# Relative-position attention and a gated FFN on one core: transposes issued directly behind the scores of their slot

## The reference

```python
q, k, v = einsum('bsx,xMnd->Mbnsd', x, qkv)
a = einsum('bnsd,bntd->bnst', q, k) * 64**-0.5
a = softmax(a + where(rel >= 0, cumsum(rpe)[:, clip(rel)], -30000), -1)
x = layernorm(x + einsum('bnsd,ndx->bsx', einsum('bnst,bntd->bnsd', a, v), out_w))
xr, xk = mix of x and the token before it, with mu_r and mu_k
x = layernorm(x + sigmoid(xr @ W_r) * (square(relu(xk @ W_k)) @ W_v))
```

## Time and profile before

| | us |
|---|---|
| median of 3 runs | 1245.39 (1245.36 to 1245.45) |
| the profiled execution's own time | 1246.39 |
| its span | 1244.6 |
| PE busy | 1118.1 (90%) |
| POOL busy | 886.9 (71%) |
| DVE busy | 843.3 (68%) |
| ACT busy | 743.1 (60%) |

### The profile page before, as it was taken

The page is one execution under the profiler, slowest core; times in us unless marked ns, Lnnn a source line. Parts: engine busy times, 40 slices in busy tenths (PEclk is TensorE's granted clock), DMA queues, the critical chain, the costliest instruction groups (busy, mean ns, idle before and its releaser), DMA issues.

```text
span 1244.6 us, 21976 instructions
## 1 busy us (share of the span) xinstructions
PE 1118.1 (90%) x6909; PEld 781.9 (63%) x6909; DVE 843.3 (68%) x2505; ACT 743.1 (60%) x1857; POOL 886.9 (71%) x527
## 2 busy tenths in 40 slices
PE   5899999999999999999999999999999999999885
PEld 3666666666666666666666666666666666666664
DVE  2666666666676767777667777666777676777746
ACT  3666666666655656656665656665656566656623
POOL 1877777878876677876677876677876677776730
PEclk9899999999999999999999999999999999999997
DMA  8855445555655455655465654456654455654600
GB/s 199 208 122 124 115 117 122 130 132 134 157 138 115 116 141 127 160 137 129 116 141 132 159 127 118 117 140 153 159 123 115 123 134 142 155 122 110 213 18 20
DMA packets 101745, 163.69 MB, mean 132 GB/s; under 512 B 10592, under 2 KB 66288, under 8 KB 101632
## 3 DMA queue, kind: packets, MB, share of 16 engines
q1 hardware_dynamic: 99472, 161.37, 53.4%
q10 hardware_dynamic: 2160, 0.92, 0.3%
HBM read 41.63 MB, written 19.96 MB: 49 GB/s over the span
## 4 chain that ended last, share of the span: by engine, by line
PE 65%; DVE 17%; issue 8%; ACT 6%; POOL 2%; DMA 1%; DVEq 0%; SPq 0%; ACTq 0%
PE ps_o L946 21%; PE ps_t L930 15%; PE ps_rows L916 13%; PE ps_m L891 7%; DVE prob L615 4%; DVE pt L632 4%; PE ps_m L960 4%; PE ps_m L896 3%; ACT pt L474 2%; DVE mix_sb L638 2%; POOL prob L410 2%; ACT prob L463 1%; DVE k_lo L601 1%; DVE q_lo L601 1%; DVE shift L682 1%
## 5 line engine op out<-in xcount | busy, mean ns | idle before, releaser
L410 POOL TENSOR_SCALAR prob<-prob,inv 128x128 f32<-128x128 f32 (+7 forms) x512 | 880.5, 1730 | 308.2 <-DVE inv L622 306.2
L463 ACT ACTIVATE prob<-prob,low 128x128 f32<-128x128 f32 (+7 forms) x512 | 395.3, 773 | 119.1 <-DVE low L615 116.9
L615 DVE CUSTOM_DVE_ANT_0 prob<-ps_rows,table 128x128 f32<-128x128 f32 (+7 forms) x512 | 383.6, 749 | 72.7 <-PE ps_rows L916 66.2
L930 PE MATMUL ps_t<-ident,prob 128*128 128x128 f32 x2304 | 349.1, 278 | 87.2 <-ACT pt L474 50.1
L916 PE MATMUL ps_rows<-stacks 128*128 128x512 f32 (+3 forms) x1536 | 402.5, 372 | 4.6 <-DVE w_t L700 3.2
L930 PEld LDWEIGHTS ps_t<-ident,prob 128*128 128x128 f32 x2304 | 260.6, 141 | 198.3 <-issue 130.6
L632 DVE COPY pt<-ps_t 128x256 f32<-128x256 f32 (+2 forms) x320 | 179.1, 568 | 179.6 <-PE ps_t L930 178.8
L474 ACT ACTIVATE pt<-ps_t 128x128 f32<-128x128 f32 (+2 forms) x448 | 203.6, 477 | 110.8 <-PE ps_t L930 110.6
L946 PE MATMUL ps_o<-pt,v_pair 128*64 128x512 f32 (+3 forms) x1536 | 268.7, 492 | 0.0
L916 PEld LDWEIGHTS ps_rows<-stacks 128*128 128x128 f32 x1536 | 246.3, 191 | 22.7 <-DVE w_t L700 3.4
L946 PEld LDWEIGHTS ps_o<-pt,v_pair 128*64 128x64 f32 x1536 | 101.8, 136 | 181.8 <-issue 172.3
(11 more groups left out here) (108 smaller groups left out, 561.6 us busy)
## 6 DMA issues: line engine op xcount, KB each, us to landing
stacks<-k_hi SPq DMA_DIRECT2D x126, 256.0 KB, 4.7
stacks<-k_lo SPq DMA_DIRECT2D x126, 256.0 KB, 4.9
stacks<-q_hi SPq DMA_DIRECT2D x63, 256.0 KB, 3.7
stacks<-q_lo SPq DMA_DIRECT2D x63, 256.0 KB, 4.4
mix_transposed<-mix_sb SPq DMA_DIRECT2D x62, 256.0 KB, 2.0
table<-bias_by_distance SPq DMA_DIRECT2D x64, 192.0 KB, 3.7
mix_tile<-mix_transposed SPq DMA_DIRECT2D x24, 512.0 KB, 5.0
w_cur<-in_L_attn_qkv SPq DMA_DIRECT2D x31, 192.0 KB, 3.9
```

What stands on the lines that cost most here:

```text
L410: nc.gpsimd.tensor_scalar(row, row, inv[:, r:r + 1], None, ALU.mult).then_inc(s_norm, 1)
L463: nc.scalar.activation(row, row, ACT.Exp, bias=low[:, r:r + 1], scale=-1.0, accum_out=total[:, r:r + 1]).then_inc(s_exp, 1)
L615: nc.vector.tensor_tensor_reduce(prob[:, r % PSLOTS, 0:width], ps_rows[:, score_at(r):score_at(r) + width], table[n % 2][:, h, 0:width][:, ...
L930: ins = nc.tensor.transpose(ps_t[k % 2][:, P * b:P * b + P], prob[:, r % PSLOTS, at:at + P], ident[:, :])
```

## The change

In each slot, PE's transposes now come directly behind the scores, ahead of the projection, the tile step and the mix burst. On ACT, the copies of transposed banks now come ahead of the projection copy and the tile step. On DVE, the copies of transposed banks come ahead of the split. No instruction is added or removed, and no size is changed.

```diff
@@ ACT step
                 for slot in range(NROWS):
+                    for k in range(NBANKS):
+                        if BANKS[k][0] == slot and EVACUATOR[k] == "1":
+                            evacuate(n, k)
                     if more and slot in PROJ_SLOTS:
                         project(n + 1, PROJ_SLOTS.index(slot))
                     if tile_too:
                         tile_step(n, slot)
-                    for k in range(NBANKS):
-                        if BANKS[k][0] == slot and EVACUATOR[k] == "1":
-                            evacuate(n, k)
                     for row in rows_ahead(n, more, slot):
                         exps(*row)
@@ DVE step
-                    if more and slot in PROJ_SLOTS[:4]:
-                        project(n + 1, PROJ_SLOTS.index(slot))
                     for k in range(NBANKS):
                         if BANKS[k][0] == slot and EVACUATOR[k] == "0":
                             evacuate(n, k)
+                    if more and slot in PROJ_SLOTS[:4]:
+                        project(n + 1, PROJ_SLOTS.index(slot))
@@ PE step
                     for row in rows_ahead(n, more, slot):
                         score(*row)
+                    transpose(n, slot)
                     if more and slot in PROJ_SLOTS:
                         project(n + 1, PROJ_SLOTS.index(slot), tile_too)
                     if tile_too:
                         tile_step(n, slot, more)
@@
                     if slot == MIX_NEAR:
                         mix(n, 0, 0, GROUP)
-                    transpose(n, slot)
```

## The result

The kernel before takes 1245.42 us (median of 4 runs, 1245.36 to 1245.9), the changed one 1235.28 (4 runs, 1233.90 to 1236.43). The ratio is 0.9917, with a 95% interval of 0.990 to 0.9934: 10.1 us faster, where 13.0 were forecast (1232.4). The profiled execution took 1236.43 us, with a span of 1234.7. Two executions of kernels further down lie far off the others of their kernel and are left out: the profiled one of e9 (1299.54 us at a granted clock of 0.847, so e9 has no idle time and no steps in the table) and one of e10 (2220.36 us).

A forecast was written before the change was run, and what follows sets the result against it. PE's order was taken to bound the kernel, its idle waits being the gain: 22 tile steps at 0.57 us (12.5) plus 0.5 for the last step, plain steps 0, made 13.0 us, so 1232.4; range 1222 to 1245.

The forecast's parts named there:

- PE bound, and what is to be won is its standing: Whole kernel: PE is busy 90% of the span; reordering can win its idle time, 87.2 us ahead of the transposes.
- Slot 0: Tile step: row 0's transposes wait 0.2 to 0.3 for ACT; output projection 0.4 later, 0.3 us taken as loss.
- Slot 4: Tile step: transpose of x1 loses cover, wait grows from 0.39 to 0.6 or 0.7; scores 9 start 0.6 us later.
- Slot 9: Tile step: row 9's transposes wait 1.2 us, FFN projections behind them cost 0.44 in full; scores 14 start 1.04 later.
- Slots 12 to 15: Tile step end: waits for bank copies go or shrink, winning 1.6 us; row 15's transposes at 636.05 for 636.62.
- POOL's floor: Tile step: POOL's run lets row 15's transposes start no sooner than 635.75, close behind the forecast's own limit.
- Plain steps: Eight steps: row 2's transposes and POOL's run 0.5 us late, POOL takes the end's win; 0, between -0.3 and +0.2.
- The gaps that repeat: Whole kernel: PE's gaps repeat step after step.
- The first (early losses don't arise): Slots 0, 4 and 9 have unseen slack, row 15's transposes stand on POOL's floor: 35 us gained, 1210; chance 0.10.
- The second (the bubbles only move): Tile steps: slots 12 to 15 win 1.0 us and the others lose 1.04, 1245 in all; chance 0.11.
- The third (lost cover costs more than the end gives back): Scores 0 to row 15's transposes shorten by under 1.04 us; at only 0.42, 14 us slower, 1259; chance 0.11.
- The add of y and x1 beside POOL's run (L682): Tile step: DVE's add at 632.66 took 0.65 us in the middle of POOL's unbroken run.

The follow-up runs named there:

- e9: e4 with row 9 inverted on DVE in slot 6 ahead of the bias of row 10: 1206.90 us, ratio 0.9699.
- e10: e9 with DVE's copy of the far mix also moved ahead of the bias of row 10: 1215.28 us, ratio 0.9761.
- e4: Changed kernel with the projections of slots 2 and 3, output projection (slot 0) and FFN projections (slot 9) again ahead of the transposes: 1208.28 us.
- e1: Kernel before with only ACT's reordering, PE and DVE in their old order: 1273.98 us, ratio 1.0239.
- e2: Kernel before with only PE's reordering, ACT and DVE in their old order: 1265.30 us, ratio 1.0172.
- e8: Changed kernel with only the projections of slots 2 and 3, and their ACT copies, again ahead of the transposes: 1220.93 us, ratio 0.9819.
- e5: Changed kernel with ACT's second layer-norm root again ahead of the copies of banks 18 and 19: 1249.79 us, ratio 1.0048.
- e6: Changed kernel with the transposes of row 11 again behind the near mix burst: 1264.52 us, ratio 1.0164.
- e3: Changed kernel without DVE's part, its splits again ahead of its copies: 1236.11 us, ratio 0.9934.
- e11: Changed kernel with y2 written to PSUM, so the add L682 has one input in SBUF: 1235.25 us, ratio 0.993.
- e12: e10 and e11 together: 1206.85 us, ratio 0.9707.

## Why the prediction held, point by point

**PE bound, and what is to be won is its standing.** Shown: over the kernels of the table the time goes up and down with the idle time ahead of the transposes and x1, to 0.7 us from before to after and to 0.2 from there to e4. It gives the direction and not always the size: e1 and e2 are 30.4 and 21.7 us slower than before with 15.5 and 10.7 more.

**Slot 0.** Said: T0 waits 0.2 to 0.3 for ACT and the output projection starts 0.3 to 0.4 later. Measured: 0.20, and 672.98 is 0.81 behind the scores where it was 0.32: 0.5 later.

**Slot 4.** Said: the wait ahead of x1 grows from 0.39 to 0.6 or 0.7, scores 9 come 0.6 later. Measured 0.72 and 0.65. e8 undoes it, and the wait is 0.3.

**Slot 9.** Said: T9 waits 1.2 and the FFN projections cost 0.44 in full, so scores 14 are 1.04 late. Measured: 1.21, and scores 0 of the next pair 1.17 late. Of the missing 0.13, 0.10 is there by T9, which starts 22.96 us into the step for 22.26 (said: 0.6 later, measured 0.70). From T9 to scores 14 it takes 1.05, as said (0.60 and 0.44), and 0.02 comes in behind them.

**Slots 12 to 15.** Said: from scores 0 to T15 5.45 us instead of 7.06. Measured: 5.45. The size is right, and so are the short waits of T13 and T14 and the root's part (e5 shows it worth 0.67 a step, e6 shows T11's place worth 0.90). T15's path is the one that was given: it starts 0.14 behind DVE's copy of bank 20, and PE's own work comes to it hardly sooner, for T15 stands 0.60 behind scores 3 where it is 0.55 in a plain step, which has no such wait (233.04 to 233.59). But to the hundredth the number is luck: DVE was ready for inversion 15 0.90 behind scores 0 and not 0.69, and came from there to the copy in 3.74 and not 3.86. Within this stretch the add took 0.29 and not 0.65, and the wait for the root, which was 0.15 and was to become 0.30, became 0.67; the second makes up for the first, since the root (706.19) now follows ACT's copies and not the add. T13 and T14 came 0.26 and 0.43 later in the step than forecast (32.54 for 32.28, 34.01 for 33.58), which DVE's stretch covered. POOL's floor was near, as said, but not touched: by the mean durations of its rows in the trace before (2.85 us for 1024 columns, 2.53 for 896, 2.21 for 768, 1.89 for 640) rows 9 to 15 take 2 x (2.85 + 2.53 + 2.21) + 1.89 = 17.07, so they end at 707.88, and T15 (708.38) came 0.35 after the 0.15 that would have had to follow.

**DVE's part.** The prediction gives DVE's reordering no term of its own, only that slots 2 and 5 keep their sum. e3, without it, has the same steps and is 0.8 us slower, less than the runs spread.

**Plain steps.** Here a term was mis-sized. Said: 0, between -0.3 and +0.2, as T2 comes 0.5 later and POOL's run takes what the end wins. Measured: +0.14, 1.1 us over 8 steps. PE, the scores of row 10 in a plain step before, whose step begins at 200.09:

```profile
213.35 1.07 PE L916 MATMUL ps_rows<-stacks 128*128 128x512 f32 x4
```

And PE in the changed kernel, whose step begins at 199.85:

```profile
200.61 0.30 PE L930 MATMUL ps_t<-ident,prob 128*128 128x128 f32 x1 [0.28 <-ACT pt L474]
...
202.21 0.52 PE L930 MATMUL ps_t<-ident,prob 128*128 128x128 f32 x3 [0.34 <-DVE pt L632]
...
213.91 1.09 PE L916 MATMUL ps_rows<-stacks 128*128 128x512 f32 x4
...
233.59 1.03 PE L930 MATMUL ps_t<-ident,prob 128*128 128x128 f32 x8
```

Scores 10 start 14.06 us into the step for 13.26: 0.8 later, not 0.5. T0 waits 0.28 for 0.16, T2 comes 0.5 late as said, and the rest comes in over slots 3 to 5. From there to the end of the step 0.66 is won back.

T15 shows no wait for POOL, which I had said would be seen, though it is abreast of it: POOL's run starts at 216.41 here, and 17.07 and 0.15 later it is 233.63, T15's own start within the error of that count. That the total came out near zero owes something to luck: the forecast had POOL's run begin 0.3 too early and, scaled by columns, gave its rows 17.4 us where their own durations add up to 17.07. e8, which puts T2's cover back, brings plain steps to 33.93.

```profile
216.41 19.69 POOL L410 TENSOR_SCALAR prob<-prob,inv 128x768 f32<-128x768 f32 x10 [1.58 <-DVE inv L622]
```

**The sum.** The add of y and x1 runs once in each tile step, so its first and last start (the two rows just below) cut the execution in three: 370.4 us became 370.7 up to the first one, the 23 steps between went from 858.1 to 848.8, and what follows the last from 16.1 to 15.2. Forecast were 0 for the first part, 23 x 0.57 = 13.1 for the second, 0 for the third; measured are -0.3, 9.3 and 0.9. So the gain is short in the tile steps: 23 x 0.13 = 3.0 because the losses are 1.17 and not 1.04, and some 1 for the few long ones. The loss of the plain steps doesn't show in the first part, where the start of the kernel took about 0.8 less; no run here says why.

**The rivals.** The first (early losses don't arise) is out: scores 10 moved by 0.67. The second (the bubbles only move) is out in the time, though half of it is in the trace: DVE's share grew by 11.4 us while ACT's shrank by 23.0. The third (lost cover costs more than the end gives back) was the near one. It decides by the length from scores 0 to T15, and e5 shows how near it was: with the root alone put back, that stretch gives back too little and the kernel is 0.5% slower than before.

**The gaps that repeat.** PE's gaps repeated from step to step. They were largely order: with the same two banks the idle time ahead of the transposes went 87.2, 70.5, 53.3 us from before to changed to e4. Whether a third bank would take the rest no run here shows.

**The add of y and x1 beside POOL's run (L682).** Here are all 24 of the kernel before, then all 24 of the changed one (ns: least, median, most; then the first and last start in us).

```profile
L682 DVE TENSOR_TENSOR shift<-y,x x24: 291/634/653, 370.4 to 1228.5; 128x128 f32<-128x128 f32 x24
```

```profile
L682 DVE TENSOR_TENSOR shift<-y,x x24: 291/292/1143, 370.7 to 1219.5; 128x128 f32<-128x128 f32 x24
```

Every add with both inputs in SBUF that began in the first 0.97 us of one of POOL's rows of 1024 columns, 118 in the profiles of ten of the kernels, ended 1.25 to 1.27 us behind the start of that row, wherever it had begun: 0.10 behind it (e10, 1.17 long), 0.61 (before, 0.65) or 0.74 (e1, 0.51). The adds that began ahead of the row, by 0.15 in the changed kernel, or 1.24 and more behind the start of a row (e4, mostly 2.02) took their 0.29. So only an add that began in the first 0.97 us of a row that lasts 2.85 took longer, not one that began 1.24 us or more into it. With one input in PSUM 24 adds began in that first part (e11, e12), and all took 0.29.

The forecast's stretch of DVE has the add at the 0.65 of before; that the change brought the add to just ahead of the row is luck. It didn't change the time of a step: the changed kernel has DVE wait 0.67 for the root behind the add, and an add of 0.65 would by that have shortened this wait by 0.36 and nothing else. e10 and e12 bear this out, where 0.87 more of the add takes 0.51 out of that wait (0.15 for 0.66) and costs the step 0.35 (36.23 for 35.88).

## What to carry to other kernels

In an in-order engine, work that needs nothing belongs in front of the instruction that waits, and the instruction whose result frees a buffer belongs ahead of those that wait for some other chain. So decide slot by slot: put the transposes first where their bank is free and another engine waits for them, and leave the filler in front where they wait themselves; the rule applied to all slots won 10 us here, with four exceptions 35. Reorder producer and consumer together: PE's half alone cost 21.7 us, ACT's alone 30.4, and both gained 7.5 to 10. And where a wait is attributed to an engine that was long done, or none is shown, look for the copy that ended 0.15 us earlier before building the next version on it. A short operation of VectorE with two inputs in SBUF, beside a run on GpSimd, took 1.14 us and not 0.29 by a shift of a quarter of a microsecond; one input in PSUM ended that.

## What the hardware showed that I had not expected

The same kernel's runs differ by up to 6 us, and in the two kernels here the difference goes with the mean granted clock: the changed kernel took 1233.90 and 1234.29 at 0.993 and 0.992, and 1236.28 and 1236.43 at 0.990; e4 took 1205.64 and 1206.99 at 0.994 and 0.993, 1209.57 and 1210.93 at 0.989. In the profiled execution of the changed kernel the clock is 1.00 from 60 to 1200 us, and lower near the start (the windows below) and at the end (0.85 behind 1200). Windows of it (busy time and count of PE, PEld, DVE, ACT, POOL, then the granted clock, the DMA share and GB/s):

```profile
10.00:20.00 10.00, 6.45 (x19) 3.01 (x19) 2.40 (x4) 3.08 (x5) 0.00 (x0) 0.83 0.93 228
20.00:30.00 10.00, 5.46 (x42) 4.69 (x40) 2.73 (x12) 5.22 (x12) 1.24 (x2) 1.00 0.82 164
30.00:40.00 10.00, 9.09 (x34) 6.88 (x35) 5.43 (x20) 5.33 (x15) 5.80 (x6) 0.66 0.92 286
...
60.00:1200.00 1140.00, 1055.92 (x6561) 737.33 (x6561) 782.51 (x2357) 719.02 (x1771) 853.52 (x497) 1.00 0.55 132
```

From 10 to 20 us, PE was busy 6.45 us, behind a start in which it waited for the first inputs (for x 3.15 us until 6.19 and 3.55 until 15.34), and the granted clock was 0.83; from 30 to 40 it was 0.66, behind ten us of which PE was busy 5.46 and the clock 1.00. That the start makes much of the spread is shown by one pair only: the profiled execution of e11 has a granted clock of 1.00 from 10 to 20 us and 0.83 from 30 to 40, and a span of 1232.1 for 1234.7. Of these 2.6 us 1.9 are there ahead of the first add (368.8 for 370.7), 0.6 in the 23 steps between the first and the last add. No run tried to hold the clock at the start.

The chains between engines had a constant in them: from the end of a copy to the transposes that wait for it, 0.14 or 0.15 us in each case worked out here.
